# LayerNorm after the expert choice moved into the biased attention, its weight splits and bias diagonals moved into the expert choice

## What is computed

```python
# expert choice: 8 experts, each takes the k = 64 tokens of a batch with the highest affinity
affinity = jnp.transpose(jax.nn.softmax(logits, axis=-1), (0, 2, 1))
gating, idx = jax.lax.top_k(affinity, k)
h = jax.nn.silu(x_in @ w_gate) * (x_in @ w_up)          # per expert, inner width 1024
out = jnp.zeros_like(x).at[bidx, idx].add(gating[..., None] * x_e)
x = _layernorm(x + out)                                  # the LayerNorm that is moved
# attention with a relative position bias: 16 heads of 64, no mask
scores = jnp.einsum('bhqd,bhkd->bhqk', q, k) + compute_bias(rel_emb, s, s)
x = _layernorm(x + softmax(scores) @ v @ wo)
```

## Time and profile before

| | us |
|---|---|
| median of 3 runs | 2056.77 |
| lowest and highest of them | 2056.28, 2057.68 |
| the profiled execution, its own time | 2067.0 |
| its span (first to last instruction) | 2064.9 |
| PE, PEld busy | 1765.3, 1417.4 |
| DVE, ACT, POOL busy | 1137.7, 1008.4, 740.0 |
| mean granted TensorE clock | 0.927 |

### The profile page before, as it was taken

The page is one execution under the profiler, slowest core; times in us unless marked ns, Lnnn a source line. Parts: engine busy times, 40 slices in busy tenths (PEclk is TensorE's granted clock), DMA queues, the critical chain, the costliest instruction groups (busy, mean ns, idle before and its releaser), DMA issues. The chain is left out here.

```text
span 2064.9 us, 40861 instructions
## 1 busy us (share of the span) xinstructions
PE 1765.3 (85%) x15132; PEld 1417.4 (69%) x15132; DVE 1137.7 (55%) x3100; ACT 1008.4 (49%) x2377; POOL 740.0 (36%) x650
## 2 busy tenths in 40 slices
PE   7988875789839999949999999778889995999994
PEld 5777664667538888836777777556567774788883
DVE  3666664456445454535555555545558772457774
...
DMA packets 97899, 125.47 MB, mean 61 GB/s; under 512 B 8586, under 2 KB 84826, under 8 KB 97674
## 3 DMA queue, kind: packets, MB, share of 16 engines
...
## 5 line engine op out<-in xcount | busy, mean ns | idle before, releaser
L2014 POOL TENSOR_TENSOR L1a_probs<-L1a_probs,L1a_rinv 128x1024 f32<-128x1024 f32 x64 | 121.2, 1894 | 270.6 <-DVE L1a_rinv L2329 270.6
L2011 POOL TENSOR_TENSOR L0a_probs<-L0a_probs,L0a_rinv 128x256 f32<-128x256 f32 (+1 forms) x128 | 103.1, 826 | 190.7 <-DVE L0a_rinv L2329 190.7
L2321 DVE CUSTOM_DVE_ANT_0 L1a_sbias<-L1a_psS,L1a_bias 128x256 f32<-128x256 f32 x256 | 93.2, 420 | 109.3 <-PE L1a_psS L2122 109.2
L2274 ACT ACTIVATE L1a_probs<-L1a_sbias,L1a_nmx 128x256 f32<-128x256 f32 x256 | 126.5, 497 | 47.6 <-DVE L1a_nmx L2321 47.6
L3001 POOL DMA_INDIRECT moe_sums<-moe_y,moe_xg x39 | 81.3, 2084 | 137.0 <-DVE moe_y L3300 113.8
L2585 POOL DMA_INDIRECT ec_sums<-ec_yk,ec_token_at x32 | 59.0, 1845 | 190.5 <-ACT ec_yk L2706 185.6
L2274 ACT ACTIVATE L0a_probs<-L0a_sbias,L0a_nmx 128x128 f32<-128x128 f32 (+1 forms) x256 | 112.8, 443 | 28.8 <-DVE L0a_nmx L2321 28.8
L2771 DVE TENSOR_TENSOR ec_h<-ec_sg,ec_psU 128x512 f32<-128x512 f32 x64 | 43.9, 687 | 120.0 <-ACT ec_sg L2693 120.0
L3079 PE MATMUL moe_psY<-moe_wts,moe_hT 128*128 (+1 forms) x440 | 104.0, 379 | 0.8 <-ACT moe_hT L3146 0.8
L2618 PE MATMUL ec_psG<-ec_xs,ec_wt 128*128 128x512 f32 x384 | 99.4, 395 | 2.1 <-issue 2.1
L2321 DVE CUSTOM_DVE_ANT_0 L0a_sbias<-L0a_psS,L0a_later 128x128 f32<-128x128 f32 (+1 forms) x256 | 76.2, 354 | 44.4 <-PE L0a_psS L2119 44.0
...
## 6 DMA issues: line engine op xcount, KB each, us to landing
...
```

Of the source, the lines that this page charges most:

```text
L2011: last = pool.tensor_tensor(v, v, bcast(rinv[:, r, :, t], 2, KEYS[t]), ALU.mult)
L2014: last = pool.tensor_tensor(v, v, bcast(rinv[:, r, :, :].rearrange("p h t -> p (h t)"), 2, S), ALU.mult)
L2274: ins = act.activation(probs[:, r, j, at], sbias[:, g % 2, j, at], ACT.Exp, bias=nmx[:, r, j, t:t + 1], scale=-1.0, accum_out=sums[:, r, j ...
L2321: last = dve.tensor_tensor_reduce(out=sbias[:, g % 2, j, at], in0=psS[:, slot + j, at], in1=added, scale=-1.0, scalar=LARGE, op0=ALU.add, ...
```

## The change

The expert choice and the attention become a pair: `expert_choice_stage` only leaves its arguments, and `expert_choice_run` is called from `attention_stage`; it hands over `shelf`, the tile `wt` and a new tile `next_v` in SBUF, and `ec_sums` in DRAM.

- Removed at the end of the expert choice: the four loads of `ec_sums`, the normalization of 16 tiles and the four stores.
- Added to the expert choice: loads of `rel_emb` and `onehot` ahead of the first weight load, their product on PE beside the top 64 selection, the ACT copy and the store of the diagonals; behind the last expert's hidden tiles three ACT copies and three DVE subtractions that split q, k and v.
- The attention reads x of each batch from `ec_sums` and normalizes it: DVE `input_stats` (2 statistics, 2 aggregates, 1 add), GpSimd `root_input` (1 power), DVE `input_shift` (1), ACT `apply_input` (2 Identity, in place). For batches 0 and 1 this stands ahead of the front part, for batch b + 2 at p = 6 and p = 7 of batch b.
- In the front part of the attention no weight is split but o: ACT copies its high part behind qk 4; GpSimd makes the low part in two halves at g = 1 and 2.
- `load_x(1)` goes out ahead of the bias loads.

```diff
         if not latent:
-            shelf_life, shelf = consts[6].pop()
+            shelf_life, split_life, shelf, wqk, wv, sums_in = held
+            ctx.callback(split_life.close)
+            x_in = sums_in.rearrange("(b t p) d -> b p t d", t=TT, p=P)
...
-            wqkv = {k: sb("w" + k, [P, 2, KD, H * HD], F32R) for k in "qkv"}
+            wqkv = {"q": wqk[:, :, 0, :, :], "k": wqk[:, :, 1, :, :], "v": wv}
...
-                sp.dma_start(emb, w["rel_emb"]).then_inc(small_in, 16)
-                sp.dma_start(onehot, w["onehot"]).then_inc(small_in, 16)
                 load_x(0)
-                sp.wait_ge(pre_taken, 1)
-                sp.dma_start(w["diag"], diag).then_inc(diag_out, 16)
-                sp.wait_ge(diag_out, 16)
+                load_x(1)
                 for n, (first, home) in enumerate(loads):
                     sp.dma_start(home, bass.AP(tensor=w["diag"].tensor, offset=first * 512,
...
-                for n, k in ((2, "v"), (3, "o")):
-                    dst = wo if k == "o" else wqkv[k]
-                    pool.wait_ge(pre_high, n + 1)
-                    pool.tensor_tensor(dst[:, 1, :, :].rearrange("p a b -> p (a b)"), raw[k],
-                                       dst[:, 0, :, :].rearrange("p a b -> p (a b)"), ALU.subtract).then_inc(lowered[n], 1)
...
+            def root_input(b):
+                pool.wait_ge(in_asked, b + 1)
+                pool.tensor_tensor(in_rstd[:], in_rstd[:], minus_half[:], ALU.pow).then_inc(in_rooted, 1)
+
+            if not latent:
+                root_input(0)
+                root_input(1)
+
+            def lower_out(half):
+                pool.wait_ge(pre_high, 1)
+                at = slice(half * KD * 512, (half + 1) * KD * 512)
+                pool.tensor_tensor(wo[:, 1, :, :].rearrange("p a b -> p (a b)")[:, at], raw_o[:, at],
+                                   wo[:, 0, :, :].rearrange("p a b -> p (a b)")[:, at], ALU.subtract).then_inc(o_lowered, 1)
...
+                if not latent and g in (1, 2):
+                    lower_out(g - 1)
+                if not latent and g % NP == 6 and g // NP + 2 < B:
+                    root_input(g // NP + 2)
...
+                    else:
+                        pe.wait_ge(x_normed, b + 1)
...
-                        pe.wait_ge(lowered[3], 1)
+                        pe.wait_ge(o_lowered, 2)
...
+                    if b == 1 and what[1] == NP // 2:
+                        act.wait_ge(o_lowered, 2)
...
+            def apply_input(b):
+                act.wait_ge(in_shifted, b + 1)
+                for t in range(TT):
+                    ins = act.activation(xb[:, b % RX, t, :], xb[:, b % RX, t, :], ACT.Identity, bias=in_shift[:, t:t + 1],
+                                         scale=in_rstd[:, t:t + 1])
+                ins.then_inc(x_normed, 1)
...
-                for k in "qkvo":
-                    if k == "k":
-                        act.wait_ge(pre_ready, 1)
-                        act.activation(diag, psT[0:H, 0, :], ACT.Copy).then_inc(pre_taken, 1)
-                    if k == "v":
-                        take(("xT",), 0)
-                    split((wo if k == "o" else wqkv[k])[:, 0, :, :].rearrange("p a b -> p (a b)"), raw[k])
+                apply_input(0)
+                take(("xT",), 0)
+                apply_input(1)
...
+                if not latent and n == 4:
+                    split(wo[:, 0, :, :].rearrange("p a b -> p (a b)"), raw_o)
...
+                if not latent and p == 7 and b + 2 < B:
+                    apply_input(b + 2)
...
+            def input_stats(b):
+                dve.wait_ge(x_in_sem[b % RX], 16 * (b // RX + 1))
+                for t in range(TT):
+                    instep.done(dve.bn_stats(in_stats[:, t, :], xb[:, b % RX, t, :]))
+                instep.wait()
+                if b:
+                    dve.wait_ge(x_normed, b)
+                for t in range(TT):
+                    instep.done(dve.bn_aggr(in_mv[:, t, :], in_stats[:, t, :]))
+                instep.wait()
+                dve.tensor_scalar(in_rstd[:], in_mv[:, :, 1], LN_EPS, None, ALU.add).then_inc(in_asked, 1)
+
+            def input_shift(b):
+                dve.wait_ge(in_rooted, b + 1)
+                dve.scalar_tensor_tensor(out=in_shift[:], in0=in_mv[:, :, 0], scalar=-1.0, in1=in_rstd[:],
+                                         op0=ALU.mult, op1=ALU.mult).then_inc(in_shifted, 1)
...
-                for n, k in ((0, "q"), (1, "k")):
-                    dve.wait_ge(pre_high, n + 1)
-                    dve.tensor_tensor(wqkv[k][:, 1, :, :].rearrange("p a b -> p (a b)"), raw[k],
-                                      wqkv[k][:, 0, :, :].rearrange("p a b -> p (a b)"), ALU.subtract).then_inc(lowered[n], 1)
+                input_stats(0)
+                input_shift(0)
+                input_stats(1)
                 take(("xT",), 0)
+                input_shift(1)
...
+                if not latent and b + 2 < B:
+                    if p == 6:
+                        input_stats(b + 2)
+                    elif p == 7:
+                        input_shift(b + 2)
...
+        split_life = ExitStack()
+        wt = split_life.enter_context(nc.sbuf_tensor("ec_wt", [P, 2, 2, KD, I], F32R, side="right"))
+        next_v = split_life.enter_context(nc.sbuf_tensor("next_v", [P, 2, KD, I], F32R, side="right"))
...
+                sp.dma_start(emb[:], follow["rel_emb"]).then_inc(small_in, 16)
+                sp.dma_start(onehot[:], follow["onehot"]).then_inc(small_in, 16)
                 load_up(0)
...
+                sp.wait_ge(diag_made, 1)
+                sp.dma_start(follow["diag"], diag[:]).then_inc(diag_out, 16)
                 for e in range(2, E):
...
-                        .then_inc(next_in, 16)
+                        .then_inc(next_in[n], 16)
+                sp.wait_ge(diag_out, 16)
+                sp.wait_ge(next_in[3], 16)
                 for s in range(ST):
                     sp.wait_ge(last_added[s], 16)
-                    sp.dma_start(acc[:, GR * s:GR * (s + 1), :],
-                                 sums[GR * s * P:GR * (s + 1) * P, :].rearrange("(t p) d -> p t d", p=P))\
-                        .then_inc(sums_loaded[s], 16)
-                for s in range(ST):
-                    sp.wait_ge(out_ready, GR * (s + 1))
-                    b = GR * s // TT
...
-                sp.wait_ge(stored, 16 * ST)
-                sp.wait_ge(next_in, 16 * 4)
...
-                pool.memset(halves[:], -0.5).then_inc(made, 1)
-                pool.wait_ge(made, 2)
...
-                for s in range(ST):
-                    pool.wait_ge(var_ready, s + 1)
-                    at = slice(GR * s, GR * (s + 1))
-                    pool.tensor_tensor(rstd[:, at], rstd[:, at], halves[:, at], ALU.pow).then_inc(rstd_ready, 1)
...
+                pe.wait_ge(small_in, 2 * 16)
+                pe.matmul(psX[0:H, 0, :], emb[:], onehot[:], start=True, stop=True).then_inc(diag_ready, 1)
...
+                pe.wait_ge(diag_made, 1)
                 turn_rows(0)
...
                 weight_high(0)
+                act.wait_ge(diag_ready, 1)
+                act.activation(diag[:], psX[0:H, 0, :], ACT.Copy).then_inc(diag_made, 1)
                 row_high(0)
...
+                    else:
+                        for n, high in enumerate(next_parts(0)):
+                            act.wait_ge(next_in[n], 16)
+                            act.activation(high, next_raw(n), ACT.Copy).then_inc(next_high, 1)
...
-                for s in range(ST):
-                    act.wait_ge(shift_ready, s + 1)
-                    for t in range(GR * s, GR * (s + 1)):
-                        act.activation(acc[:, t, :], acc[:, t, :], ACT.Identity, bias=shift[:, t:t + 1],
-                                       scale=rstd[:, t:t + 1]).then_inc(out_ready, 1)
...
-                def center(s):
-                    at = slice(GR * s, GR * (s + 1))
-                    dve.wait_ge(rstd_ready, s + 1)
-                    dve.scalar_tensor_tensor(out=shift[:, at], in0=mv[:, at, 0], scalar=-1.0, in1=rstd[:, at],
-                                             op0=ALU.mult, op1=ALU.mult).then_inc(shift_ready, 1)
-
-                step = Chain(dve, ln_step, 0)
-                for s in range(ST):
-                    at = slice(GR * s, GR * (s + 1))
-                    dve.wait_ge(sums_loaded[s], 16)
-                    for t in range(GR * s, GR * (s + 1)):
-                        step.done(dve.bn_stats(stats[:, t, :], acc[:, t, :]))
-                    step.wait()
...
-                    dve.tensor_scalar(rstd[:, at], mv[:, at, 1], LN_EPS, None, ALU.add).then_inc(var_ready, 1)
-                    if s:
-                        center(s - 1)
-                center(ST - 1)
-    consts[6].append((shelf_life, shelf))
+                    else:
+                        for n, (high, low) in enumerate(zip(next_parts(0), next_parts(1))):
```

(4 more changed lines are left out.)

70 lines of the change are left out of this document (33 added, 37 removed).

## The result

Three series were timed, each beside the kernel before:

| series | runs | changed, median | before, median | ratio, 95% interval | difference of means (standard error) |
|---|---|---|---|---|---|
| first | 20, 20 | 2052.65 | 2057.84 | 0.9960, 0.9942 to 0.9977 | -8.3 (1.7) |
| second | 8, 25 | 2069.56 | 2084.99 | 0.9937, 0.9914 to 0.9961 | -14.4 (2.3) |
| third | 6, 11 | 2068.53 | 2085.07 | 0.9926, 0.9903 to 0.9949 | -15.6 (2.3) |

What follows compares the result with a forecast made beforehand. PE bounds the attention loop, but at the border between the stages it idles 19.07 us, so what leaves there shortens the kernel in full. -14.6 - 0.4 + 0.1 = -14.9 takes 2056.77 to 2041.9 us; range 2038.5 to 2047.5.

Steps and rivals of the forecast that it cites:

- Part 1: End of the expert choice: LayerNorm's loads, tiles and stores go, and the last landing may come sooner; -14.6 us.
- The stage now ends when SyncE has seen the last addition land: Border: landing seen at 889.49, attention's first instruction 1.17 later at 890.66 in place of 904.77; -14.11 us.
- its start and the fourth's at 884.62 stay: Expert 7's third and fourth GpSimd additions keep their starts, idle time absorbing the ACT copies' 1.2 us delay; cost 0.
- the whole -1.03: Fourth addition's landing 3.84 after its issue, without loads beside it; between 0 and -1.03, taken as -0.5 us.
- Part 2: Attention up to qk 0: LayerNorm of batch 0 takes what the splits leave, 9.17 for 9.56; -0.4, range -1.4 to +2.7.
- Part 3: Splits moved or left: ACT's o copy costs 0 (bound +1.9), GpSimd's two halves of o +0.1 us.
- Part 4: Start of the expert choice: small loads and bias diagonals hide behind existing waits; 0, from -0.1 to +0.8 us.
- Part 5: Attention loop, batches 2 to 7: LayerNorm pieces fit idle gaps; 0, bound +6.6 us.
- B: Rival: LayerNorm work in the attention loop is exposed, all six times giving -8.3, 2048.5 us; chance 0.07.
- D: Rival: slower, ACT reloads tables for Identity at p = 7 of six batches, +22.0, 2063.9 us; chance 0.03.
- Rival A: Attention's front part gives some back, by late x of batch 0 or exposed o split; typically -12, 2044.8; chance 0.12.
- The range: Forecast interval for the whole kernel's median, 2038.5 to 2047.5 us.

Runs made afterwards that it cites:

- pool_late: Changed kernel with GpSimd also waiting for the last landing and filling a small tile at the expert choice's end; four stages from expert choice to last attention 1116.3 us.
- no_sub: Changed kernel with expert 7's three VectorE subtractions replaced by zero fills of the low parts; four stages from expert choice to last attention 1110.4 us.
- splits_back: Changed kernel with q, k and v split in the attention again, LayerNorm and bias diagonals still moved; 2073.65 us, ratio 0.9959.
- ln_back: Changed kernel with LayerNorm, its loads and stores at the end of the expert choice again, none in the attention; 2079.24 us, ratio 0.9966.
- before_again: The kernel before, traced once more without edit; four stages from expert choice to last attention 1124.2 us.
- waits_back: Changed kernel with PE's long satisfied waits put back, 20 in a batch, as before the change; four stages from expert choice to last attention 1110.5 us.
- best_warm_38: Changed kernel plus v split among expert 7's products, x of batch 0 loaded beside GpSimd's drain, and unread PE products (38 behind expert 7); 2063.54 us, ratio 0.9905.
- again: The changed kernel run and traced a second time without edit; four stages from expert choice to last attention 1112.6 us.
- again_2: The changed kernel run and traced a third time without edit; four stages from expert choice to last attention 1112.6 us.

## Why the prediction was wrong

**Part 1, -14.6, measured -11.1 (448.47 to 437.39 in the expert choice; 904.77 to 893.35 is -11.4, but 0.3 of that came from the stages ahead). This is the step that failed.** Its sentence "The stage now ends when SyncE has seen the last addition land", with 1.17 from there to the first instruction, left out GpSimd's own drain. From the landing seen at 889.4 to 893.35 it is 3.95: +2.78. I had read the 1.17 off a border at which GpSimd's drain was over at 903.0, before SyncE was done at 903.60; it said nothing of a border that GpSimd ends. pool_late shows the drain by itself. The other sentence that failed is "its start and the fourth's at 884.62 stay": the copies moved the first issue by 0.9 where 1.2 was worked out, and no_sub shows that this alone leaves the fourth in its place, but VectorE's subtraction stretched the first issue by 1.9, of which the idle time left ahead of the third addition could take 0.6 (no_sub has 0.90 there, and 0.30 is the least). That is +1.28 counted from the stage's start; no_sub and splits_back show its cause. The subtractions were priced as free because they end 8 us ahead of the border; what they hold up stood beside them, not behind. The landing 3.84 after its issue gave the whole -1.03, of which I had taken half. The rule of the Trainium skill (DMA: Bandwidth & Descriptors, Issuing engines are not separate DMA queues), by which the whole of it comes, agrees with the 3.84. Ledger: -14.11 + 1.28 - 1.03 + 2.78 = -11.08.

**Part 2, -0.4, measured -0.88.** x landed 2.66 after the first instruction and not 3.23, in spite of its new neighbours. The LayerNorm chain took 3.49 for 3.48.

**Part 3, +0.1, measured about 0.** GpSimd's halves of o took 2.39 and 2.41, dearer than the 1.90 taken. The scaling behind the first still had 1.82 of idle time; the one behind the second had none, but began at 953.46, 0.08 after its input was there (953.38), as the others do.

**Part 4, 0, measured 0.** In splits_back, which keeps the moved diagonals, the fourth addition starts at the same 428.3 after the stage's start as before.

**Part 5, 0, measured 0 for the LayerNorm.** ln_back shows it; the transposes wait for nothing new and there is one table load, so B and D are off. Not foreseen: the batch is shorter by 0.34, mostly because the q and k weights lie elsewhere. The seven intervals of the loop give -2.7, but 0.7 of it is the last one, which before_again has as short as the changed kernel (31.49).

**What was not in the sum.** Front and loop together brought the biased attention to 436.1 from 441.1 or 438.9, but the three stages behind the border are the same to 0.5 in two traces of three: the last attention runs 2.5 longer, with 37.5 us at 1.2 GHz and not 30.7. So the border alone, -11.1, comes near the -11.5 of the four stages and the -11.8 of the three series, by gains and losses behind it that cancel. Rival A had put the sum near -12, but neither of its causes, a late x and an exposed split of o, appeared: its number is near by luck. What makes the clock fall more in that stage is not settled; no_sub, waits_back and best_warm_38 show it at 171.3 to 171.6 with the same code, so it depends on what comes before.

The range also failed on its second ground: it took the median of three runs, 2056.77, for the level, and allowed nothing for the scatter of the series. Its lower and upper end stood 9 us apart; the first series alone has a difference of -8.3 (-5.2 by its medians) where the two later ones have -14.4 and -15.6. The failed step explains 3.5 of what was missing, -11.1 for -14.6. The rest of the distance from -14.9 to the first series' -5.2 no trace explains, and that the two later series lie near -14.9 does not save the working: again and again_2, traced in them, have the same expert choice of 437.5 and 437.4, and with it the same failed step. The 4 us that I took for what a measurement can tell was too little as well. Of the mechanism, what was right is that the border shrinks by most of its length and nothing in the loop pays; what was wrong is which engine ends it.
